# Graph network kernel on one Trainium2 core: the first group's convolution taken from unsplit fp32 operands

## The reference

```python
xc = jnp.transpose(x, (0, 2, 1))
h = _bn(_conv1d(xc, conv1_w, 0), bn1_g, bn1_b, bn1_m, bn1_v)
h = jax.nn.relu(h)
h = _bn(_conv1d(h, conv2_w, 8), bn2_g, bn2_b, bn2_m, bn2_v)
x_conv = jnp.transpose(jax.nn.relu(h + xc), (0, 2, 1))
s = x @ w_se.T + b_se
...
A = jnp.exp(-dist) * mask
msg = jax.nn.relu(x @ w_msg.T + b_msg)
x_nmp = jnp.einsum('bnm,bmd->bnd', A, msg)
x_in = jnp.concatenate([x_conv, x_nmp], axis=-1)
```

## Time and profile before

| | before |
|---|---|
| median of 3 runs | 409.75 us (409.53 to 411.69) |
| profiled execution, its own time | 410.32 us |
| span in the profile | 408.5 us |
| TensorE busy | 379.7 us, 93% |
| DVE busy | 283.9 us, 69% |
| ACT busy | 235.9 us, 58% |
| POOL busy | 234.7 us, 57% |

### The profile page before, as it was taken

One profiled execution on the slowest core, in us unless ns is written; L12 is line 12 of the kernel. 1 busy time (PEld: TensorE's weight loads), 2 busy tenths in 40 slices (PEclk: granted clock), 3 DMA queues, 4 the chain that ended last, 5 costly groups with the idle time before them and its releaser, 6 DMA issues.

```text
span 408.5 us, 6677 instructions
## 1 busy us (share of the span) xinstructions
PE 379.7 (93%) x2369; PEld 339.2 (83%) x2369; DVE 283.9 (69%) x548; ACT 235.9 (58%) x430; POOL 234.7 (57%) x219
## 2 busy tenths in 40 slices
PE   2697899999999999999999999999999999999783
PEld 2687788899898988899898998989898998988773
DVE  5899748867587647876588666885588665855653
ACT  3664256646665477546756378456756477353933
POOL 2698814848356645748348465657349464664332
PEclk9998899999999999999999999999999999999989
DMA  7402001111012010021012010120112010000101
GB/s 254 177 2 103 2 1 51 55 51 51 0 54 104 0 54 22 34 100 39 12 51 103 0 51 0 51 103 18 35 53 103 2 51 2 1 2 0 53 0 51
DMA packets 7991, 19.39 MB, mean 47 GB/s; under 512 B 672, under 2 KB 5024, under 8 KB 6944
## 3 DMA queue, kind: packets, MB, share of 16 engines
q1 hardware_dynamic: 7536, 18.50, 12.8%
q10 hardware_dynamic: 432, 0.59, 0.5%
HBM read 14.89 MB, written 4.19 MB: 47 GB/s over the span
## 4 chain that ended last, share of the span: by engine, by line
PE 62%; DVE 20%; issue 6%; ACT 6%; POOL 4%; DMA 1%; DVEq 0%; ACTq 0%; SPq 0%; POOLq 0%
PE back L1115 28%; PE conv L1115 16%; PE front L1191 7%; PE back L1278 6%; POOL rstd L478 4%; DVE xn L934 3%; DVE wl L966 3%; PE front L1163 2%; DVE usum L883 2%; DVE stl L803 2%; DVE esum L877 2%; DVE usum L865 1%; DVE gbuf L898 1%; ACT tail L674 1%; DVE stats L912 1%
## 5 line engine op out<-in xcount | busy, mean ns | idle before, releaser
L1115 PE MATMUL conv<-sth,wh 128*128 128x256 f32 x320 | 98.2, 307 | 8.6 <-issue 3.6
L1115 PE MATMUL conv<-sth,wl 128*128 128x256 f32 x320 | 92.4, 289 | 0.0
L1115 PE MATMUL conv<-stl,wh 128*128 128x256 f32 x320 | 92.4, 289 | 0.0
L478 POOL TENSOR_TENSOR rstd<-rstd,minus_half 128x4 f32<-128x4 f32 (+1 forms) x34 | 36.1, 1062 | 67.1 <-DVE rstd L916 67.1
L1115 PEld LDWEIGHTS conv<-sth,wh 128*128 128x128 f32 x320 | 61.6, 192 | 11.3 <-issue 5.5
L1115 PEld LDWEIGHTS conv<-stl,wh 128*128 128x128 f32 x320 | 61.8, 193 | 1.0
L1115 PEld LDWEIGHTS conv<-sth,wl 128*128 128x128 f32 x320 | 61.7, 193 | 0.0
L483 POOL TENSOR_TENSOR xw<-xw,xv 128x512 f32<-128x512 f32 (+1 forms) x17 | 20.9, 1228 | 63.5 <-ACT xw L658 63.5
L496 POOL TENSOR_TENSOR amat<-amat,adjT 128x512 f32<-128x512 f32 x32 | 48.3, 1530 | 0.8
L665 ACT ACTIVATE xch<-usum 128x512 fp32r<-128x512 f32 x16 | 10.1, 631 | 39.1 <-DVE usum L883 39.1
L1191 PE MATMUL front<-amat,msg 128*128 128x256 f32 x128 | 30.4, 380 | 0.0
(11 more groups left out here) (201 smaller groups left out, 1002.2 us busy)
## 6 DMA issues: line engine op xcount, KB each, us to landing
adjT<-in_adj_dram SPq DMA_DIRECT2D x8, 1024.0 KB, 4.8
out_dram<-tail SPq DMA_DIRECT2D x15, 256.0 KB, 2.2
xv<-in_x_dram SPq DMA_DIRECT2D x7, 512.0 KB, 3.3
gbuf<-in_gates_dram SPq DMA_DIRECT2D x1, 576.0 KB, 6.4
tail<-in_conv_dram ACTq DMA_DIRECT2D x2, 256.0 KB, 3.8
xv<-in_x_dram SPq DMA_DIRECT2D x2, 256.0 KB, 4.6
later_w<-in_later_dram SPq DMA_DIRECT2D x1, 452.0 KB, 6.1
tail<-in_conv_dram SPq DMA_DIRECT2D x1, 320.0 KB, 5.2
```

The lines of the kernel that those rows point to most:

```text
L478: done(pool.tensor_tensor(rstd[:, k, h, q], rstd[:, k, h, q], minus_half[:, q], ALU.pow), RSTD[k])
L1115: ins = pe.matmul(bank, a, b, start=first and k == 0, stop=last and k == len(todo) - 1)
```

## The change

Group 0's 40 tap products are taken from the unsplit fp32 streams and the unsplit tap sums (`first_taps`), so no parts of either are needed for them. `dx0` gives each stream a buffer of its own for its differences: `dx` for M, and for A and B space in `xn` and `xw`, which the back of group 0 uses only later. The three pairs of `odd_low` and `diff_low` and of `odd_high` and `diff_high` of group 0 go (`stage(..., first=1)` counts from group 1). The parts of the weights are still made, in the order `W_ORDER`: subs 0, 1, 2, then gates and `W1`, then 3 and 6, and at the end of the prologue 4, 5, 7, 8. TensorE waits for them at three places of `steady(1)` (`first`). The low parts of the gates' weights and of `W1` move from POOL to DVE. On ACT the Relus of the messages move forward, on POOL a tap sum moves to the front.

```diff
+        dx0 = [dx] + [t.rearrange("p (k b t) -> p k b t", k=2, b=GB) for t in
+                      (xn[:, :, :, :].rearrange("p h q d -> p (h q d)")[:, 0:2 * GB * TL],
+                       xw[:, :, :].rearrange("p h n -> p (h n)")[:, 0:2 * GB * TL])]
+        W_ORDER = ("conv1", 0, 1, 2, "gates", "w1", 3, 6, 4, 5, 7, 8)
+        def w_count(name):
+            return W_ORDER.index(name) + 1
```

On SP, in the prologue:

```diff
                 wait(sp, A_READY, 0, 1)
-                sp.wait_ge(w_low, 10)
+                wait(sp, CONV_FULL[6], 0, 1)
+                sp.wait_ge(w_low, w_count(6))
                 load_adj(1, 1)
```

On POOL, `first_diff` and the prologue:

```diff
+            def first_diff(st):
+                ev, od = stream_even(st), stream_odd(st)
...
+                done(pool.tensor_tensor(dx0[st][:, 0, :, :], ev, od, ALU.subtract), DX_READY[st])
+                done(pool.tensor_tensor(dx0[st][:, 1, :, :], one_on(ev), od, ALU.subtract), DX_READY[st])
...
-                split_diff(0, 0)
                 pool.wait_ge(conv2_loaded, 64)
                 pool.tensor_tensor(qsum[:, 5:9, :], c2raw[:, 0:TAPS - 1:4, :], c2raw[:, 2:TAPS:4, :],
                                    ALU.add).then_inc(tap_sums_ab, 1)
+                first_diff(0)
                 diff_a(0)
-                split_diff(0, 1)
+                first_diff(1)
+                diff_b(0)
                 pool.tensor_tensor(qsum[:, 10:14, :], c2raw[:, 1:TAPS:4, :], c2raw[:, 3:TAPS:4, :],
                                    ALU.add).then_inc(tap_sums_ab, 1)
-                diff_b(0)
-                mask(0, 0, 0)
-                mask(0, 0, 1)
-                split_diff(0, 2)
-                mask(0, 0, 2)
-                mask(0, 0, 3)
+                first_diff(2)
+                for b in range(GB):
+                    mask(0, 0, b)
+                wait(pool, CONV_FULL[2], 0, 1)
                 split_diff(1, 0)
-                pool.wait_ge(w_high, 11)
-                pool.tensor_tensor(wl[:, S_GATE:S_GATE + 9, :], graw, full(wh[:, S_GATE:S_GATE + 9, :]),
-                                   ALU.subtract).then_inc(w_gate_low, 1)
-                pool.wait_ge(w_high, 12)
-                pool.tensor_tensor(w1l[:, :], w1raw, full(w1h[:, :]), ALU.subtract).then_inc(w_gate_low, 1)
+                wait(pool, CONV_FULL[4], 0, 1)
                 diff_a(1)
                 split_diff(1, 1)
+                wait(pool, CONV_FULL[7], 0, 1)
                 diff_b(1)
```

On DVE, the prologue from the first messages on:

```diff
+                for k in range(3):
+                    messages(0, k)
+                factors(0)
                 tap_low(0)
...
                 x_low(1, 1, 0)
                 x_low(1, 1, 1)
+                tap_low(1)
+                tap_low(2)
+                m_sum(0)
+                w_low_part(wl[:, S_GATE:S_GATE + 9, :], graw, wh[:, S_GATE:S_GATE + 9, :], w_count("gates"))
+                w_low_part(w1l[:, :], w1raw, w1h[:, :], w_count("w1"))
                 x_sum(0, 0, 0)
                 x_sum(0, 0, 1)
                 g_sum(0, 0)
                 pre_sum(0, 0)
+                tap_low(3)
+                tap_low(6)
                 odd_low(1, 0)
+                xconv_low(0, 0)
                 diff_low(1, 0)
                 nmp_low(0, 0)
...
                 g_sum(0, 1)
                 pre_sum(0, 1)
+                nmp_low(0, 1)
                 xconv_low(0, 1)
+                tap_low(4)
+                tap_low(5)
+                tap_low(7)
+                tap_low(8)
```

On TensorE:

```diff
+            def first_taps(n):
+                st, kind = n // 3, n % 3
...
+                src = stream_odd(st) if kind == 0 else dx0[st][:, kind - 1, :, :]
+                bank = conv_half(n).rearrange("p (b t) -> p b t", t=TQ)
+                for k in range(NTAP[n]):
+                    ins = pe.matmul(bank, traw[n][:, k, :], src[:, :, k:k + TQ], start=k == 0, stop=k == NTAP[n] - 1)
+                done(ins, CONV_FULL[n])
...
-                pe.wait_ge(w_low, 2)
-                taps(0, 0)
+                first_taps(0)
+                first_taps(1)
                 pe.wait_ge(consts_loaded, 16)
                 factors(0)
-                pe.wait_ge(w_low, 3)
-                taps(0, 1)
+                first_taps(2)
                 distances(0, 0)
                 distances(0, 1)
-                pe.wait_ge(w_low, 4)
-                taps(0, 2)
+                first_taps(3)
...
             def steady(s, u, front):
                 gb, gm, gf, ub = s - 1, s, s + 1, 1 - u
+                first = isinstance(s, int) and s == 1
+                if first:
+                    pe.wait_ge(w_low, w_count(2))
                 taps(gm, 0)
                 taps(gm, 1)
                 taps(gm, 2)
                 messages(gm, u)
+                if first:
+                    pe.wait_ge(w_low, w_count("w1"))
                 gates(gb, ub, 0)
...
                 y_transpose(gb, 0)
+                if first:
+                    pe.wait_ge(w_low, w_count(8))
                 taps(gm, 3)
```

More of the change, by code:

```diff
@@ L184, in gnn_kernel, with stage @@
         count = {}
-        def stage(name, per_group):
-            count[name] = (sem(name), per_group)
+        def stage(name, per_group, first=0):
+            count[name] = (sem(name), per_group, first)
             return name
@@ L199, in gnn_kernel @@
         DX_READY = [stage(f"diff{n}_split_ready", 2) for n in "MAB"]
-        STH_READY = [stage(f"stream{n}_high_ready", 2) for n in "MAB"]
-        ST_READY = [stage(f"stream{n}_ready", 2) for n in "MAB"]
+        STH_READY = [stage(f"stream{n}_high_ready", 2, 1) for n in "MAB"]
+        ST_READY = [stage(f"stream{n}_ready", 2, 1) for n in "MAB"]
         CONV_FULL = [stage(f"sub{n}_full", 1) for n in range(9)]
@@ L280, in gnn_kernel @@
         w_low = sem("w_low")
-        w_gate_low = sem("w_gate_low")
         tap_sums_ab = sem("tap_sums_ab")
         def wait(eng, name, g, j):
-            s, per = count[name]
-            v = g * per + j
+            s, per, first = count[name]
+            v = (g - first) * per + j
             if not (isinstance(v, int) and v <= 0):
@@ L291, in done @@
         def done(ins, name):
-            s, per = count[name]
+            s, per, _ = count[name]
             ins.then_inc(s, 16 if per == 16 else 1)
@@ L462, in split_diff @@
                 done(pool.tensor_tensor(dx[:, 1, :, :], one_on(ev), od, ALU.subtract), DX_READY[st])
+            def first_diff(st):
+                ev, od = stream_even(st), stream_odd(st)
+                if st == 0:
+                    wait(pool, H1_READY, 0, 2)
+                else:
+                    wait(pool, DV_READY, 0, (1, 3)[st - 1])
+                done(pool.tensor_tensor(dx0[st][:, 0, :, :], ev, od, ALU.subtract), DX_READY[st])
+                done(pool.tensor_tensor(dx0[st][:, 1, :, :], one_on(ev), od, ALU.subtract), DX_READY[st])
             def diff_a(g):
@@ L701, in prologue @@
                 h1_out(0, 1)
-                odd_high(0, 0)
                 act.wait_ge(tap_sums, 1)
                 tap_high(0)
-                tap_high(1)
-                diff_high(0, 0)
-                tap_high(2)
-                act.wait_ge(tap_sums_ab, 1)
-                tap_high(3)
-                odd_high(0, 1)
-                factors_out(0)
-                tap_high(4)
-                tap_high(5)
-                mm_out(0)
-                exps(0, 0)
-                exps(0, 1)
-                diff_high(0, 1)
-                x_high(1, 1)
-                exps(0, 2)
-                exps(0, 3)
-                act.wait_ge(tap_sums_ab, 2)
-                tap_high(6)
-                tap_high(7)
-                tap_high(8)
-                odd_high(0, 2)
-                am_out(0)
                 for k in range(3):
                     msg_out(0, k)
-                diff_high(0, 2)
+                tap_high(1)
+                mm_out(0)
+                x_high(1, 1)
+                factors_out(0)
+                tap_high(2)
+                for b in range(GB):
+                    exps(0, b)
                 act.wait_ge(gates_loaded, 16)
                 act.activation(wh[:, S_GATE:S_GATE + 9, :], graw, ACT.Copy).then_inc(w_high, 1)
+                act.activation(w1h[:, :], w1raw, ACT.Copy).then_inc(w_high, 1)
+                am_out(0)
+                act.wait_ge(tap_sums_ab, 2)
+                tap_high(3)
+                tap_high(6)
+                wait(act, CONV_FULL[0], 0, 1)
                 h1_out(1, 0, True)
@@ L734, in prologue @@
                 odd_high(1, 0)
+                xconv_high(0, 0)
                 bm_out(0)
-                act.activation(w1h[:, :], w1raw, ACT.Copy).then_inc(w_high, 1)
-                xconv_high(0, 0)
                 diff_high(1, 0)
@@ L741, in prologue @@
                 xconv_high(0, 1)
+                tap_high(4)
+                tap_high(5)
+                tap_high(7)
+                tap_high(8)
             def steady(s, u, front):
@@ L1024, in prologue @@
                 pre_sum(0, 0)
+                tap_low(3)
+                tap_low(6)
```

(24 more changed lines are left out.)

41 lines of the change are left out of this document (7 added, 34 removed).

## The result

| | before | after |
|---|---|---|
| median of the runs | 410.51 us (6 runs, 409.53 to 411.69) | 399.91 us (6 runs, 399.66 to 401.61) |
| ratio to before | | 0.975 (0.9725 to 0.9776) |
| span of the profiled execution | 408.5 us | 398.0 us |
| sub 1 of group 1 starts | 46.63 | 38.02 |
| sub 3 of group 1 starts | 66.65 | 56.66 |

The account below looks back on a forecast made before the run. TensorE bounds the steady groups, but DVE's stream up to g_sum(0, 1) delays sub 1 of group 1. 8.9 us earlier, 1.6 low clock gone, 0.5 new wait: 10.0 us less, median 399.8 us, range 398.2 to 403.8.

Parts of the forecast that it names:

- The number: Whole kernel: 10.0 us less, a forecast median of 399.8 us from 409.75.
- The bound: DVE's stream to g_sum(0, 1) delays sub 1 of group 1 until 46.63 us; groups behind are TensorE's work.
- TensorE's own work: From 12.2 us, TensorE's instructions take 25.5 us, so sub 1 of group 1 could start at 37.7.
- DVE up to `g_sum`: DVE's prologue stream: 24.1 + 8.8 + 4.4 for POOL's share, so g_sum(0, 1) ends at 37.3 us.
- DVE's long wait for ACT's copy of the gates' weights: In the prologue, DVE's gates' low part waits for ACT's copy, which ends at 24.1 us.
- b to c: From sub 1 to sub 3 of group 1: 20.02 us before, 1.6 low clock gone, 0.5 wait added.
- low clock: Matmuls from sub 1 of group 1 on: 4.96 us would become 3.33, saving 1.6 us.
- new wait: In group 1's first gates, TensorE waits 0.3 to 0.6 us, as DVE's deferred low parts precede the messages' evictions.
- The sum: Up to sub 3 of group 1: 8.9 earlier, 1.6 low clock gone, 0.5 new wait, 10.0 us less.
- the messages hide POOL's earlier tap sum: At the start, four-tap sums come at 11.3 instead of 10.3 us, hidden by TensorE's messages until 12.2.
- The clock did not fall in group 1: Rival: the clock falls once more in group 1, the 1.6 us stay, 401.4 us; chance 0.08.
- The rule of a lock without overlap: Rival: DVE and POOL never overlap in the prologue, costing 1.4 us, 401.2 us; chance 0.08.

Follow-up runs that it names:

- e4: Changed kernel with two more additions of 512 columns on DVE right before g_sum(0, 1): 402.79 us.
- e5: Changed kernel with five more additions of 512 columns on DVE right before g_sum(0, 1): 407.19 us.
- e7: Changed kernel with one tap product fewer in each of subs 4 to 8 of group 0, so the convolution is incomplete: 401.17 us.
- e10: Changed kernel with POOL's first tap sum moved behind its first differences, plus six early plain products on zeros on TensorE: 400.07 us.
- e11: Changed kernel measured once more, unchanged: 400.38 us.
- e2: Changed kernel with all three streams of group 0 taking their differences in one buffer again, masks interleaved: 403.74 us.
- e3: Changed kernel with the low parts of the gates' weights and W1 made by POOL again, behind the masks: 401.80 us.
- e9: Changed kernel with POOL's first tap sum moved behind its first differences, which wait for DVE's four-tap sums: 400.63 us.
- e6: Changed kernel with four more plain products of 256 columns on TensorE behind sub 5: 402.68 us.
- e8: Changed kernel with six plain products on zeros on TensorE ahead of the first convolution: 402.45 us.
- e1: Changed kernel with the low parts of subs 4, 5, 7, 8 made early again, not at the prologue's end: 403.61 us.

## Why the prediction was right

- *The number.* That 399.8 was met to 0.1 us is in part luck. The forecast subtracted 10.0 us from 409.75, the median of three runs; the six runs of the result have 410.51, and the change gave 10.6. The two differences cancel.
- *The bound.* That DVE's stream held back sub 1 of group 1 and that all behind it is TensorE's work: right. With the change all executions need 322.1 to 322.5 us from sub 3 of group 1 to the restart near the end (before: 322.9, 0.5 us more; half of it lies at one place, where the transposes at 350.69 us start 0.39 us behind the product ahead of them, 0.12 in the changed kernel, and no run explains it).
- *TensorE's own work.* Forecast 25.5 us from 12.2 to 37.7; measured 25.92, to 38.02. Plain products 0.434 for 0.433. What was too small is the messages' end in some executions, since the clock rose later there.
- *DVE up to `g_sum`.* Forecast 37.3, measured 37.36. e4, e5 and e7 bear out that this chain is the second one, within about a microsecond. The way there was another than described. The sum starts at 24.1 us with DVE's long wait for ACT's copy of the gates' weights, and there was no such wait: DVE, busy all the time, got to that low part just as the copy ended (24.38), so that its own work, which the sum did not count, set the start as well. ACT and DVE there:

```profile
23.21 1.17 ACT L729 ACTIVATE wh<-gbuf 128x1152 fp32r<-128x1152 f32 x1
```

```profile
23.54 0.74 DVE L866 SCALAR_TENSOR_TENSOR esum<-conv,bn,mms 128x512 f32<-128x512 f32 x1
24.40 1.57 DVE L973 TENSOR_TENSOR wl<-gbuf,wh 128x1152 fp32r<-128x1152 f32 x1
```

  That the two came together is luck. Part of this uncounted work is `factors`, which took 3.4 us beside POOL's differences. Its results were ready at 16.45, just ahead of TensorE's transposes at 16.60; in e10 and e11 TensorE waited 0.4 us for them:

```profile
13.00 1.15 DVE L844 SCALAR_TENSOR_TENSOR halfsq<-fact 128x24 f32<-128x24 f32 x1
...
14.42 0.60 DVE L852 CAST facthl<-fact 128x80 fp32r<-128x80 f32 x1
15.05 0.72 DVE L854 TENSOR_TENSOR facthl<-fact,facthl 128x80 fp32r<-128x80 f32 x1
15.69 0.76 DVE L856 CAST facthl<-facthl 128x80 fp32r<-128x80 f32 x1
```

- *b to c.* Forecast 1.6 us of low clock gone and 0.5 of new wait, 1.1 net; measured 20.02 - 18.64 = 1.38. The low clock was worth 1.4 (4.99 or 4.96 against 3.55), the wait in the gates 0.1 in the profiled execution and 0.3 in e2, e3, e7, e9 and e10. Both terms were too large, and the errors partly cancel.
- *The sum.* 8.6 + 1.4 = 10.0 us at sub 3 of group 1, as forecast; the missing 0.5 between 10.0 and the 10.5 of the spans is the unexplained one above.
- *The start.* The step that says the messages hide POOL's earlier tap sum is the weakest: true in the profiled execution and in e11, not in e3, e4 and e5, where TensorE waited up to 1.2 us. The time at the low level in `messages`, which in e6 made them 0.9 us longer, has no term of its own. Neither took a run of the changed kernel itself out of the range: the longest, in e11, is 401.66.
- *Rivals.* The clock did not fall in group 1. The argument for that rival's small chance, that it fell both times after gaps of about 2 us, left out a third gap in the same trace, of 2.53 us, after which it did not fall (below). The Trainium skill's section that it names there agrees on the cause only, since the gaps it has in mind are longer than the 1.97 and 2.31 us that were enough here. The rule of a lock without overlap, of the Trainium skill's page SBUF — State Buffer ("Who interferes with whom"), again came out slightly too strict: in e5 an addition beside POOL's took 1.15 us, 0.2 less than 0.61 + 0.73, the two alone from start to start. All but for this they exclude each other, in e5 and in e8 alike.

What stays open: why c to d was 0.5 us longer before; what e1 would give with the same a and the same end as the changed kernel, since only its pieces were compared; what the plain products give without the deferring or the deferring without them; and what lets the low level of the clock last longer in some executions, at the start and at the end.

## What to carry to other kernels

A prologue that prepares split operands while the tensor engine waits can take its first products from the unsplit ones: here a plain fp32 product costs 0.43 us against 0.37 for a split one of three matmuls, and what it saves is two conversions ahead of every product, on engines that are the bound there. Once that is done two chains of nearly the same length are left, and each further saving on one of them alone comes back only in part, as e7 and e10 show. Where DVE and POOL share a stretch, their orders have to be read as one list: an instruction put on POOL costs DVE nearly its own length, and where POOL's next instructions get in between, as in e8, a chain of four took 5.4 us in place of 2.2.

## What was not expected of the hardware

- The end of the kernel has two lengths, 18.8 to 19.0 and 20.0 to 20.3 us, by how long the low clock lasts after the 3.9 us gap near the end. In the changed kernel's trace and in e7's, which has the longer end (stretches; the clock is the third number from the right):

```profile
378.00:382.00 4.00, 2.94 (x9) 2.44 (x10) 3.33 (x11) 0.00 (x0) 2.47 (x3) 0.68 0.00 0
382.00:386.00 4.00, 4.00 (x18) 3.32 (x18) 1.54 (x3) 2.03 (x4) 1.52 (x3) 0.90 0.01 4
```

```profile
378.00:382.00 4.00, 3.25 (x9) 2.71 (x10) 2.97 (x10) 0.00 (x0) 2.54 (x3) 0.50 0.00 0
382.00:386.00 4.00, 4.00 (x13) 3.22 (x13) 1.14 (x3) 1.36 (x3) 1.47 (x3) 0.67 0.00 0
```

  Worked out from these rows, the first runs at the low level for 3.4 of its 8 us, the second for 6.6. A microsecond of difference between two kernels' medians here can be this alone.
- The clock fell around TensorE's gaps of 1.97, 2.31, 2.63, 3.9 and 4.4 us, and did not at those of 1.8, 1.4, 1.2, 1.0 and 0.8. The length of the gap alone does not decide it: the kernel before has one of 2.53 us, between the messages and the first split product, and the matmuls behind it start 0.12 us apart, the pace of the high level:

```profile
14.74 0.36 PE L1115 MATMUL conv<-sth,wh 128*128 128x256 f32 x1 [2.53 <-issue]
```

- Matmuls on zeros brought the clock up too: behind six products on them the first convolution ran at 2.4 GHz (e8, e10). This agrees with the Trainium skill, TensorE: Matmul & The Clock Gate, "What's actually happening", where activity releases the throttle; products on zeros were enough here.
- DVE's COPY of 128 columns took 1.30 us behind a POOL instruction, 0.22 alone: operations with a single source are held up too.
